# TensorE's six middle attention batches written out one after another instead of looping on the engine

## The chip, the cores and the metric

The kernel runs on one core of a Trainium2 chip. A core has a matrix engine (TensorE, PE in the profile, with a row of its own, PEld, for its weight loads), a vector engine (VectorE, DVE), a scalar engine (ScalarE, ACT), a general engine (GpSimd, POOL) and an engine that issues transfers (SyncE, SP). Each runs its own program and they meet through semaphores. Every engine fetches its instructions from memory, over DMA queues that the profile lists as kind "instruction". The metric is the device time of one execution in microseconds (us); lower is better.

## The reference, cut to what matters

Eight batches of 256 tokens with 512 features pass through one decoder layer: causal attention with 32 query heads in 8 groups, a mixing stage over a second input with long convolutions, and a gated feed-forward stage with ternary weights.

```python
def reference(x, ctx_2048, ...):
    x = x + _L0_attn_ref(_layernorm(x), Wq, Wk, Wv, Wo, bo)
    x = x + _L0_xattn_ref(ctx_2048, ctx_2048, _layernorm(x), ssm_kernel, D, 8)
    x = x + _L0_ffn_ref(_layernorm(x), w_gate_up, w_proj)
    return x

# the attention
q = _rope((h @ Wq).reshape(N, S, 32, 64).transpose(0, 2, 1, 3))
k = _rope((h @ Wk).reshape(N, S, 8, 64).transpose(0, 2, 1, 3))
v = (h @ Wv).reshape(N, S, 8, 64).transpose(0, 2, 1, 3)
scores = (q @ k.T + alibi) / math.sqrt(64)
scores = 30.0 * jnp.tanh(scores / 30.0)
probs = jax.nn.softmax(jnp.where(causal, scores, -jnp.inf), axis=-1)
return (probs @ v) @ Wo + bo
```

## The kernel before

Every engine's program has three stages in a row: attention, mixing, feed-forward. Attention takes up the first 690 us and goes batch by batch. In each engine's program batch 0 is written out (`first_batch`), batches 1 to 6 are one body `attend(b)` in a loop on the engine (`Fori(1, B - 1)`, B is 8), and batch 7 is written out again (`last_batch`). A loop on the engine means that the body's instructions stand in memory once, a register counts, and a compare-and-branch at the end goes back to the head.

TensorE's body for batch b has ten steps, one for each of the eight head groups and two more:

- steps 0 and 1: the values of this batch (`project_values`, at L701 to L703 with the tile `hT_halves` as stationary side, shown as `bank<-w_hi,hT_halves`), each followed by the scores of a head group (`scores`, L779 and L782);
- steps 2 to 4: the last three of the batch's ten projections of keys and queries ("units", `project`, L701 to L703, shown as `bank<-hT_halves,w_hi`), a head group's scores, and the weighting of values for the head group two steps before (`values`, L789, L791, with the softmax sums at L814 and L816);
- steps 5 to 9: the output projection of a head group (`output`, L701 to L703 on `ctx_hi`), with scores and values as long as there are any;
- then the first seven units of batch b + 1, with the last three output projections between them. So the next batch's operands are under way when the next pass of the body begins.

What TensorE waits for in the body: `ctx_lo` (GpSimd, L2002, its last piece of a head group's context) before an output projection, `hT_in` (transposing transfers that SyncE issues at L605, from `parts` to `hT_halves`) before the first unit of the next batch, and for the scores `unit_turned` (VectorE, L1443 to L1446, the rotation of a unit), `unit_in` (the unit's transfers into `q_both`, `q_high`, `k_high`, `k_low`) and `tanh_done`.

GpSimd has the longest list per head group: it masks the exponentials (L1989), adds key sums (L1998), adds a unit's rotated parts (L1984) and makes `ctx_lo` (L2002). VectorE quantises a share of the feed-forward weights beside the attention: L1574 before the end of the body, L1579 to L1583 in step 0, L1590 in step 2.

Inside the loop a wait's target depends on the batch, so it comes from a register; the program holds small register instructions for it. Two later stages also loop on TensorE: the mixing at L987 and the feed-forward at L1104.

Of the kernel before, what the change touches and what calls it, by code (L numbers as in the profile page):

```python
# [35 lines left out]
B, S, D = 8, 256, 512  # L36
# [53 lines left out]
def decoder_layer(nc, x, ctx_pairs, wq, wk, wv, wo, bo, kern, dcoef, w_gu, w_p, rope_cos, rope_sin, key_bias, query_bias,  # L90
# [17 lines left out]
    with ExitStack() as stack:  # L108
# [587 lines left out]
        def _(pe):  # L696
# [143 lines left out]
            def attend(b):  # L840
                for step in range(STEPS):
                    filler(b, step)
                    if step < NG:
                        scores(b, step)
                    if step >= 2:
                        values(b, step - 2, False)
                pe.wait_ge(tanh_done, NG * (b + 1))
                left = range(STEPS - WO_AFTER, NG)
                for n in range(EARLY):
                    project(b + 1, n)  # L850
                    if n < len(left):
                        output(b, left[n])
# [95 lines left out]
                        output(0, g)  # L948

            first_batch()  # L950
            with pe.Fori(1, B - 1) as b:
                attend(b)
            last_batch()

# [1263 lines left out]
```

## Time and profile before

| | before |
|---|---|
| median of 3 runs | 1197.77 us (1191.97 to 1198.88) |
| the profiled execution | 1198.49 us |
| span in its profile | 1196.8 us |
| PE busy | 1139.7 us, 95% |
| PEld busy | 810.7 us, 68% |
| DVE busy | 876.6 us, 73% |
| POOL busy | 676.9 us, 57% |
| ACT busy | 553.8 us, 46% |
| mean granted TensorE clock | 0.987 |

The span is the stretch from the first to the last instruction of the profiled execution, and 1.7 us of its time lie around it. Times inside the trace count from the span's start. "Issue" as a releaser means that the engine waited for nothing that the profile shows. The granted clock is 1.0 for 2.4 GHz and 0.5 for 1.2 GHz; a stretch that has some of both shows a value between.

### The profile page before, as it was taken

To read this page: it belongs to the slowest core of one execution; us is meant where nothing else is said; L and a number is where in the kernel's file an instruction comes from. 1 tells how busy PE (TensorE), PEld (TensorE's weight loads), DVE (VectorE), ACT (ScalarE), POOL (GpSimd) and SP (SyncE) were. 2 spreads that over 40 slices of the span, in tenths; PEclk is the share of its full clock that TensorE was granted. 3 is DMA by queue.
4 is the path that set the end of the run, shared out by engine and by line. 5 is a ranking of instruction groups with operands and counts; after the bars stand their busy time and mean duration, and the time that the engine had idled before them with its cause. 6 is when DMAs were issued, how large, how long until landed. Compare 5 with 4: busy or idle time off the path is not lost. (4 is left out here: it accounts for less than half of the span.)

```text
span 1196.8 us, 27182 instructions
## 1 busy us (share of the span) xinstructions
PE 1139.7 (95%) x10867; PEld 810.7 (68%) x10882; DVE 876.6 (73%) x1287; ACT 553.8 (46%) x617; POOL 676.9 (57%) x557
## 2 busy tenths in 40 slices
PE   5998999999999999999999999999999999999998
PEld 4665557656666666566566577777786876786683
DVE  6979788687786886886878678888746645754654
ACT  6866564653754655646546500000244533542441
POOL 1553594674764945946749769999443322422331
PEclk9999999999999999999999999999999999999999
DMA  9572454464345344634544557774001222012000
GB/s 329 151 226 81 120 173 110 131 181 129 109 148 173 99 145 147 182 111 121 163 128 131 213 96 147 145 144 92 1 19 21 34 54 53 7 45 53 19 19 36
DMA packets 166191, 134.28 MB, mean 112 GB/s; under 512 B 69628, under 2 KB 127362, under 8 KB 166082
## 3 DMA queue, kind: packets, MB, share of 16 engines
q1 hardware_dynamic: 141128, 126.44, 37.0%
q10 hardware_dynamic: 24960, 6.29, 3.6%
q8 instruction: 86, 1.41, 0.5%
q14 instruction: 17, 0.14, 0.0%
HBM read 81.76 MB, written 35.21 MB: 98 GB/s over the span
## 5 line engine op out<-in xcount | busy, mean ns | idle before, releaser
L701 PE MATMUL bank<-hT_halves,w_hi 128*128 128x256 f16 x640 | 176.6, 276 | 10.4 <-DMA hT_halves<-parts 5.8
L1984 POOL TENSOR_TENSOR parts<-parts 128x512 f32<-128x512 f32 x80 | 119.2, 1493 | 105.7 <-DVE parts L1446 105.7
L703 PE MATMUL bank<-hT_halves,w_lo 128*128 128x256 f16 x640 | 176.3, 276 | 0.0
L702 PE MATMUL bank<-hT_halves,w_hi 128*128 128x256 f16 x640 | 176.3, 275 | 0.0
L963 PE MATMUL bank<-kv,toep 128*128 128x288 f32 (+2 forms) x660 | 157.8, 401 | 0.7 <-ACT qT L1211 0.5
L963 PEld LDWEIGHTS bank<-kv,toep 128*128 128x128 f32 x660 | 123.7, 190 | 34.0 <-ACT qT L1211 0.7
L2002 POOL TENSOR_TENSOR ctx_lo<-ctx,ctx_hi 128x512 f16<-128x512 f32 x64 | 105.9, 1654 | 66.2 <-ACT ctx_hi L1153 66.1
L1174 ACT ACTIVATE region_c<-bank,cap_scale 128x1536 f32<-128x1536 f32 x64 | 98.6, 1541 | 86.4 <-PE bank L782 86.0
L1989 POOL TENSOR_SCALAR_AFFINE_SELECT region_c<-region_c 128x512 f32<-128x512 f32 x128 | 86.0, 695 | 85.4 <-ACT region_c L1177 85.2
L2132 POOL TENSOR_TENSOR sqsum<-sqsum,toep 128x512 f32<-128x512 f32 x56 | 78.0, 1393 | 95.5 <-ACT toep L1353 95.3
L1041 PE MATMUL bank<-odd_halves,guT 128*128 128x256 f16 x512 | 112.2, 273 | 0.0
L1042 PE MATMUL bank<-odd_halves,guT 128*128 128x256 f16 x512 | 112.2, 273 | 0.0
L1041 PE MATMUL bank<-cpair,guT 128*128 128x256 f16 x496 | 108.8, 273 | 0.3 <-DVE hid L1863 0.3
L1042 PE MATMUL bank<-cpair,guT 128*128 128x256 f16 x496 | 108.8, 273 | 0.0
L1159 ACT CAST halves<-parts 128x512 f16<-128x512 f32 x80 | 49.2, 615 | 123.8 <-POOL parts L1984 119.4
L701 PE MATMUL bank<-region_o,ctx_hi 128*128 128x512 f16 x256 | 97.6, 381 | 6.9 <-POOL ctx_lo L2002 6.9
L1365 ACT ACTIVATE silu<-bank 128x512 f32<-128x512 f32 x64 | 38.1, 595 | 142.0 <-PE bank L1042 138.7
L1998 POOL TENSOR_TENSOR key_sum<-region_c 128x512 f32<-128x512 f32 x56 | 98.8, 1764 | 1.8
L1598 DVE TENSOR_TENSOR halves<-parts,halves 128x512 f16<-128x512 f32 x80 | 68.1, 851 | 40.5 <-ACT halves L1159 40.4
L702 PE MATMUL bank<-region_o,ctx_hi 128*128 128x512 f16 x256 | 97.3, 380 | 0.0
L703 PE MATMUL bank<-region_o,ctx_lo 128*128 128x512 f16 x256 | 97.1, 379 | 0.0
L1177 ACT ACTIVATE region_c<-region_c 128x1536 f32<-128x1536 f32 x64 | 95.1, 1485 | 2.0
(192 smaller groups left out, 2637.0 us busy)
## 6 DMA issues: line engine op xcount, KB each, us to landing
unit_halves<-halves SPq DMA_DIRECT2D x80, 256.0 KB, 2.4
q_both<-unit_halves SPq DMA_DIRECT2D x64, 256.0 KB, 2.9
q_high<-unit_halves SPq DMA_DIRECT2D x64, 128.0 KB, 3.1
toep<-kernel_padded SPq DMA_DIRECT2D x32, 256.0 KB, 4.0
wffn<-w_gu SPq DMA_DIRECT2D x6, 1280.0 KB, 6.7
cpair<-ctx_pairs SPq DMA_DIRECT2D x32, 176.0 KB, 4.8
xin<-x SPq DMA_DIRECT2D x8, 512.0 KB, 4.1
region_o<-wq SPq DMA_DIRECT2D x4, 1024.0 KB, 11.2
```

Of the source, the lines that this page charges most:

```text
L701: pe.matmul(dst, lh, rh, start=first and k == 0, stop=False)
L702: pe.matmul(dst, lh, rl, start=False, stop=False)
L703: mm = pe.matmul(dst, ll, rh, start=False, stop=last and k == n - 1)
L963: mm = pe.matmul(dst, toep[:, n, d * P:(d + 1) * P], kv[:, p, m * B + batches.start:m * B + batches.stop, :], start=(m == 0), stop=(m == l))
L1041: pe.matmul(dst, guT[:, k, col:col + P], h3_hi[p][:, k, :], start=(k == 0), stop=False)
L1042: mm = pe.matmul(dst, guT[:, k, col:col + P], h3_lo[p][:, k, :], start=False, stop=(k == DB - 1))
L1174: act.activation(s.rearrange("p (n c) -> p n c", n=3), bank[:, 0:3, :], ACT.Tanh, scale=cap_scale[:, g // 2:g // 2 + 1]).then_inc(tanh_don ...
L1177: act.activation(s, s, ACT.Exp, scale=CAP).then_inc(exp_done, 1)
L1984: pool.tensor_tensor(slot[:, 0], slot[:, 0], slot[:, 1], ALU.add).then_inc(unit_summed, 1)
L1989: last = pool.affine_select(s, s, pattern=[[0, REP], [sign, P]], compare_op=ALU.is_ge, fill=0.0, base=0, channel_multiplier=-sign)
L1998: pool.tensor_tensor(key_sum[:, g % 2], sc_first[:, g % 3, :, P:S], sc_second[:, g % 3], ALU.add).then_inc(keys_added, 1)
L2002: pool.tensor_tensor(ctx_lo[:, 2 * g:2 * g + 2, :], ctx32[:, g % 2], ctx_hi[:, 2 * g:2 * g + 2, :], ALU.subtract).then_inc(ctx_lo_done, 1)
```

## The change

```diff
@@ -948,7 +948,7 @@
             first_batch()
-            with pe.Fori(1, B - 1) as b:
+            for b in range(1, B - 1):
                 attend(b)
             last_batch()
```

`b` is now a Python number, so the body is written into TensorE's program six times, and every wait gets a constant. The instructions of the other four engines are the same, in the same order; each of them still loops. TensorE's matmuls and their order are the same too.

At the end of the body, TensorE before: the last matmuls of the seventh unit of the next batch, the loop's counter and branch, and behind them the first values matmuls of `last_batch`.

```order
L701 MATMUL bank<-hT_halves,w_hi 128x256
L702 MATMUL bank<-hT_halves,w_hi 128x256
L703 MATMUL bank<-hT_halves,w_lo 128x256
L951 REGISTER_ALU
L951 COMPARE_AND_BRANCH
L701 MATMUL bank<-w_hi,hT_halves 128x512 [waits wo_undone]
L702 MATMUL bank<-w_lo,hT_halves 128x512
```

The same place in TensorE's program of the change, between batches 1 and 2:

```order
L701 MATMUL bank<-hT_halves,w_hi 128x256
L702 MATMUL bank<-hT_halves,w_hi 128x256
L703 MATMUL bank<-hT_halves,w_lo 128x256
L701 MATMUL bank<-w_hi,hT_halves 128x512 [waits wo_undone]
L702 MATMUL bank<-w_lo,hT_halves 128x512
```

The counter and the branch are gone; the next batch's first matmul stands directly behind.

At the first scores of a batch, TensorE, the difference between the two programs:

```order
 L703 MATMUL bank<-w_hi,hT_halves 128x512
-L755 ISA
-L756 REGISTER_ALU [waits unit_in0]
-L760 ISA [waits unit_in1]
-L779 MATMUL bank<-q_both,k_high 32x2x160 [waits unit_turned]
+L779 MATMUL bank<-q_both,k_high 32x2x160 [waits unit_turned,unit_in1,unit_in0]
 L779 MATMUL bank<-q_both,k_high 32x2x192
```

The register instructions that worked out and carried waits are gone, and the matmul itself carries them all.

## Rows read from the trace of the kernel before

**Rows 1.** Page, part 1: busy time, share, instructions of TensorE.

```profile
PE 1139.7 (95%) x10867; PEld 810.7 (68%) x10882; DVE 876.6 (73%) x1287; ACT 553.8 (46%) x617; POOL 676.9 (57%) x557
```

**Rows 2.** Waits of TensorE: line, releaser: us in total, times, longest.

```profile
PE bank L701 <- issue: 12.9, 5, 2.9
...
PE bank L701 <- POOL ctx_lo L2002: 6.9, 10, 1.4
PE bank L701 <- DMA hT_halves<-parts: 5.8, 6, 2.1
```

**Rows 3.** Branches of TensorE's three loops: ns min/median/max, first and last start us.

```profile
L951 PEldq COMPARE_BRANCH  x6: 83/4242/4757, 207.5 to 619.4; - x6
...
L987 PEldq COMPARE_BRANCH  x6: 76/208/233, 726.2 to 823.2; - x6
...
L1104 PEldq COMPARE_BRANCH  x2: 76/144/211, 1005.9 to 1090.3; - x2
```

**Rows 4.** Timeline of TensorE, end of batch 3: start us, us, instruction, idle before.

```profile
373.35 0.27 PE L703 MATMUL bank<-hT_halves,w_lo 128*128 128x256 f16 x1
376.55 0.61 PE L701 MATMUL bank<-w_hi,hT_halves 128*128 128x512 f16 x1 [2.92 <-issue]
```

**Rows 5.** Windows at the five loop-backs: us, busy PE PEld DVE ACT POOL, clock, DMA.

```profile
209.31:211.78 2.47, 0.16 (x2) 0.00 (x1) 2.47 (x5) 0.62 (x1) 0.58 (x2) 1.00 0.41 126
...
536.36:539.05 2.69, 0.17 (x2) 0.00 (x1) 1.95 (x4) 0.62 (x1) 1.76 (x2) 1.00 0.54 136
sum 13.69, PE 0.82 PEld 0.02 DVE 10.28 ACT 3.09 POOL 8.17; mean PE 0.16 PEld 0.00 DVE 2.06 ACT 0.62 POOL 1.63
```

**Rows 6.** Windows, batches 1 to 7, from first values matmul to end of second scores.

```profile
130.66:138.26 7.60, 7.60 (x74) 3.74 (x73) 7.49 (x7) 3.52 (x3) 0.47 (x1) 1.00 0.49 135
211.78:221.08 9.30, 9.29 (x73) 4.15 (x74) 5.96 (x5) 4.13 (x4) 1.81 (x2) 0.82 0.84 252
295.11:304.01 8.90, 8.90 (x73) 4.08 (x74) 5.75 (x4) 4.13 (x4) 0.75 (x2) 0.85 0.86 265
376.55:385.65 9.10, 9.10 (x72) 4.10 (x72) 5.75 (x4) 4.13 (x4) 0.62 (x2) 0.83 0.81 255
457.59:466.89 9.30, 9.30 (x73) 4.14 (x74) 5.75 (x4) 4.13 (x4) 1.29 (x2) 0.82 0.80 254
539.05:548.25 9.20, 9.20 (x72) 4.07 (x72) 5.75 (x4) 4.13 (x4) 1.02 (x2) 0.81 0.76 235
621.19:628.79 7.60, 7.60 (x75) 3.73 (x73) 5.48 (x7) 4.64 (x5) 2.82 (x3) 1.00 0.72 213
```

**Rows 7.** Windows, batches 1 and 3, from first values matmul to next batch's first unit.

```profile
130.66:183.19 52.53, 50.27 (x734) 31.69 (x732) 43.61 (x64) 34.64 (x31) 40.98 (x36) 1.00 0.51 141
295.11:347.33 52.22, 51.51 (x732) 32.01 (x732) 39.73 (x60) 35.24 (x32) 39.07 (x37) 0.97 0.53 158
```

**Rows 8.** Waits of TensorE within 130 to 211 us (batch 1).

```profile
PE bank L701 <- POOL ctx_lo L2002: 1.3, 2, 1.1
PE bank L701 <- DMA hT_halves<-parts: 0.9, 1, 0.9
```

**Rows 9.** Waits of TensorE within 295 to 376 us (batch 3).

```profile
PE bank L701 <- POOL ctx_lo L2002: 0.4, 1, 0.4
PE bank L701 <- DMA hT_halves<-parts: 0.3, 1, 0.3
```

**Rows 10.** Timeline of GpSimd, first masks and key sums, batches 1 and 3.

```profile
137.79 3.32 POOL L1989 TENSOR_SCALAR_AFFINE_SELECT region_c<-region_c 128x512 f32<-128x512 f32 x2 [11.44 <-ACT region_c L1177]
...
303.55 1.22 POOL L1989 TENSOR_SCALAR_AFFINE_SELECT region_c<-region_c 128x512 f32<-128x512 f32 x2 [8.15 <-ACT region_c L1177]
```

**Rows 11.** DMA queue of instructions: count, MB, share; branch 371.62:376.38, batch 295.11:376.55, loop 706:823.

```profile
q8 instruction: 1, 0.02, 1.3%
...
q8 instruction: 9, 0.15, 0.8%
...
q8 instruction: 1, 0.02, 0.1%
```

**Rows 12.** Timelines at the loop's exit: VectorE's seventh rotation, TensorE's first scores after.

```profile
622.33 0.41 DVE L1446 TENSOR_TENSOR parts<-bank,sin_s 128x256 f32<-128x256 f32 x1
...
623.87 0.67 PE L779 MATMUL bank<-q_both,k_high 128*32 128x320 f16 x12
```

## The prediction

> **What bounds the kernel now.** I began with the busy times on the page. TensorE is busy 95% of the span, the next engine, VectorE, 73% [rows 1]. So time goes away only where TensorE idles or works at the lower clock, and the second view is the list of its waits. The largest entry in it is not a wait for another engine: 12.9 us in 5 pieces, released by "issue", each before a matmul at L701 [rows 2]. Five is the number of times that a loop of six passes goes back to its head.
>
> The third view confirms the place. The loop's branch at L951 was executed six times, 83 ns at the least and 4242 ns at the median. The two other loops of TensorE have branches of 76 to 233 ns [rows 3]. Six passes mean five taken branches and one that falls through, so I read the five long ones as taken and the 83 ns one, at 619.4 us, as the exit. The timeline at the end of batch 3 shows what reaches the array: the last matmul of the seventh unit starts at 373.35 and the next batch's first one at 376.55, with 2.92 us idle [rows 4]. TensorE had work queued, which hides part of each branch; the rest is the gap.
>
> Why this branch is long can be read from the instruction queue, at least in part. While the branch of batch 3 was pending, one block of instructions was fetched; a whole batch fetches nine, for all engines together; the loop at L987, whose body is short, needed one over its whole 117 us [rows 11]. So the attention body is fetched anew in each pass, and at the branch its head has to come from memory before anything can be issued. The short loop's body stays where it is.
>
> **What the change does, part by part.** First, it removes the branch. The gap itself, counted from where the next matmul would have started at the normal distance, is 2.47 us at the first loop-back and 2.69 us at the last, and 13.69 us over all five [rows 5]. I take that sum and not the 12.9 us of the waits, since those count from the matmuls' modelled ends.
>
> The nearest row for the price of the boundary without a loop-back is the loop's exit. There the same matmuls follow each other from the loop's last pass into `last_batch`, and the first values and scores of batch 7 take 7.60 us with nothing between [rows 6]. The change makes the five other boundaries like it. Removal: −13.7 us, if nothing that was hidden behind the gap becomes late.
>
> What could be late is the seventh unit. Scores of the next batch wait for its rotation. At the exit, the rotation's last piece ends at 622.33 + 0.41 = 622.74, and the first scores start at 623.87 [rows 12]: 1.1 us to spare without any gap. The value projection covers it. I add nothing. That projection lasts 623.87 − 621.19 = 2.7 us [rows 6, 12]; without it the scores would come 1.6 us too early, but it stays where it is.
>
> Second, the clock. In batches 2 to 6, the first values and scores take 9.30, 8.90, 9.10, 9.30 and 9.20 us, at a mean granted clock of 0.81 to 0.85; in batches 1 and 7, which no gap precedes, 7.60 us at 1.00 [rows 6]. So after each gap TensorE runs for a while at the lower of its two levels, 1.2 GHz, and loses 1.7 + 1.3 + 1.5 + 1.7 + 1.6 = 7.8 us in all. The gap is the only thing the five have in front of them and the two have not, so the drop should go with it.
>
> Is that 7.8 us a gain? Here I compare batch 1, which starts without a gap, with batch 3, which starts slow. From the first values matmul to the first unit of the next batch, batch 1 takes 52.53 us at clock 1.00 and batch 3 takes 52.22 us at 0.97 [rows 7]. The head start of 1.3 us is gone by then. It went into waits: batch 1 waits 1.3 us for `ctx_lo` and 0.9 us for the transposed inputs, batch 3 0.4 and 0.3 us [rows 8, 9]. The difference is 1.5 us, which is the head start. GpSimd explains the first part: its first two masks take 3.32 us in batch 1 and 1.22 us in batch 3 [rows 10], because in batch 1 they come while VectorE is still in its quantising steps. The wait for the inputs is that for a chain over VectorE, GpSimd, ScalarE and a transfer, which does not start earlier because TensorE's first matmuls were quick. With the gap gone, VectorE's quantising stands relative to TensorE where it stands in batch 1. So I book the clock at nothing: 7.8 us less work for TensorE, 7.8 us more waiting. Bounds: 0 and −7.8 us.
>
> Third, the register instructions before waits. They are issued by the sequencer while the array has work queued. Batch 7, written out with constants, and batch 1, in the loop with registers, both take 7.60 us for the same matmuls [rows 6]. That includes the place shown in the program's difference. Price: 0.
>
> Fourth, the code. It grows by five bodies, but TensorE executes no more instructions than before, and a body was fetched in each pass already [rows 11]. No wait on "issue" stands anywhere in TensorE's list in the middle of a body; all are at the loop-backs [rows 2]. So sequential fetching keeps up with this stream. Price: 0.
>
> The sum: 1198.49 − 13.7 = 1184.8 us for the profiled execution. That one lies 0.7 us above the median of the runs, so the median should come to 1197.77 − 13.7 = **1184.1 us**.
>
> One rule speaks against all this. The Trainium skill, page "Advanced Engine Details and Errata", section "Control Flow Timing", puts a compare-and-branch at about 108 ns; by it five of them would be worth an estimated 0.5 us, and the time would be 1197.2 us. The branches at L987 and L1104 bear it out and L951 does not, at 4242 ns. The page "Runtime: NRT & Kernel Launch", section "Instruction fetch mechanics", says that a taken branch to code which is not held forces a fetch before execution goes on, and that fetching in sequence is mostly hidden. By that rule, the trace agrees for L951, and it gives the same sum as mine.
>
> **The rivals.**
>
> (B) The clock's 7.8 us are gained as well. For it: TensorE is the busiest engine, and every step moves on with it; the 0.9 us wait for inputs in batch 1 may be chance, since such waits vary up to 2.1 us [rows 2]. Against: batch 1 [rows 7]. Time: 1184.1 − 7.8 = 1176.3 us.
>
> (C) The gap's time comes back as waits for the inputs. TensorE waits for the transposed inputs in all six batches, 5.8 us in total and 2.1 us at the most [rows 2]. They share the DMA engines with the loads of weights and with stores. If each of the six waits came to 2.1 us, that would be 12.6 − 5.8 = 6.8 us more: 1190.9 us. For it: all six already wait, so there is no slack there. Against: those transfers are issued behind work that is itself counted from the batch's start.
>
> (D) The change doesn't do what it says: the pause sits at the batch boundary for another reason than the branch, and stays. That gives 1197.8 us, or 1197.3 us with the branch's own 0.1 us each taken off. Against it: the exit at 619.4 us is the same boundary without a pause [rows 3, 6].
>
> (E) Slower: the written-out code is fetched too late. If each of 9 fetches in five batches [rows 11] stopped TensorE as long as a loop-back does on average, 13.69 / 5 = 2.7 us, it would cost 45 × 2.7 = 123 us, and the time would be 1198 − 14 + 123 = 1307 us. It decides from 13.7 / 45 = 0.30 us per fetch on. Against it: the body passes as many fetches now with no wait on "issue" in between.
>
> **How the numbers follow.** Forecast (A) 0.60, (B) 0.15, (C) 0.18, (D) 0.05, (E) 0.02. The likeliest case gives the time, 1184.1 us, and its own spread is about ±3 us, as input waits and single clock drops fall differently in each execution. The range goes from just above (B) to near (C): 1177 to 1190 us. It leaves out (D), (E), the far half of (B) and the end of (C), which is less than 2 in 10. A measurement of this kernel can tell about 1% from no change, which is 12.0 us, so the border lies at 1185.8 us. Of (A) three quarters are below it, 0.45; with (B)'s 0.15 and 0.02 of (C), faster is 0.62. The rest of (A), 0.15, of (C), 0.16, and (D) make 0.36 for within 1%. Slower is 0.02.
>
> **What would show it.** In the changed profile, TensorE's list has no "issue" wait at L701 from 130 to 620 us: that is step one. The first values and scores of every batch take 7.6 us at clock 1.00: step two. The waits for `ctx_lo` and for the inputs in batches 2 to 6 rise together by some 7 us, and each batch takes about 209.31 − 130.66 = 78.65 us from values to values, as batch 1 does up to its gap [rows 5, 6]: step three. The count of instruction fetches is about as before and none stops TensorE: step four. The prediction is wrong if "issue" waits show up inside the written-out batches, if input waits of 2 us stand in nearly every batch, or if batches take 77 us because the clock's share is kept.

## The result, and the profile after

The changed kernel takes 1186.58 us, median of six runs (1181.91 to 1190.98), against 1195.47 us for six runs of the kernel before. The ratio is 0.992, with a 95% interval from 0.990 to 0.995: 0.8% or 9.3 us less by the ratio, 8.9 us by the two medians. A second measurement gave 1185.36 us and 0.993 (0.990 to 0.995). So it is faster beyond the measurement's uncertainty, but by less than 1%, which the forecast held to be the less likely case (0.36 against 0.62). The forecast was 13.7 us less, 1184.1 us, in a range from 1177 to 1190.

The page of the changed kernel, busy times. TensorE's share is 95% as before [rows 1], in a span of 1184.8 us:

```profile
PE 1131.4 (95%) x10882; PEld 810.0 (68%) x10882; DVE 881.1 (74%) x1287; ACT 553.0 (47%) x617; POOL 687.7 (58%) x557
```

TensorE's waits in the changed kernel, whole program (line, releaser, us in total, times, longest):

```profile
PE bank L701 <- POOL ctx_lo L2002: 12.5, 14, 1.6
...
PE bank L701 <- DMA hT_halves<-parts: 8.3, 6, 2.8
```

The entry of L701 on "issue" is gone. The other two were 6.9 and 5.8 us [rows 2]: 8.1 us of waiting have come up in their place.

Windows of the changed kernel over the first values and scores of batches 1, 2, 3 and 7 (us, busy PE, PEld, DVE, ACT, POOL, granted clock, DMA share, GB/s). They answer to [rows 6]:

```profile
132.97:140.57 7.60, 7.60 (x74) 3.73 (x73) 7.50 (x7) 3.52 (x3) 0.46 (x1) 1.00 0.48 142
211.17:218.77 7.60, 7.60 (x74) 3.70 (x71) 5.68 (x8) 4.26 (x5) 1.93 (x2) 1.00 0.76 226
292.39:299.99 7.60, 7.60 (x75) 3.74 (x73) 5.47 (x7) 4.65 (x5) 2.83 (x3) 1.00 0.89 273
609.01:616.61 7.60, 7.60 (x75) 3.74 (x73) 5.47 (x7) 4.65 (x5) 2.82 (x3) 1.00 0.71 209
```

All are alike, at the full clock, and so are batches 4 to 6, which also take 7.60 us each. The same view from a batch's first values matmul to the next batch's first unit, batches 1 to 6; it answers to [rows 7]:

```profile
132.97:185.06 52.09, 50.24 (x733) 31.80 (x732) 43.58 (x64) 34.59 (x31) 40.99 (x36) 1.00 0.48 141
211.17:266.29 55.12, 50.22 (x735) 31.78 (x733) 44.15 (x65) 35.99 (x33) 44.02 (x39) 1.00 0.57 162
292.39:345.26 52.87, 50.25 (x734) 31.78 (x732) 41.92 (x64) 35.75 (x33) 43.52 (x38) 1.00 0.59 173
371.37:424.63 53.26, 50.22 (x735) 31.73 (x733) 43.88 (x65) 35.97 (x33) 43.75 (x39) 1.00 0.57 167
450.73:503.22 52.49, 50.24 (x735) 31.81 (x732) 41.89 (x64) 35.71 (x33) 43.50 (x38) 1.00 0.59 168
529.33:582.91 53.58, 50.23 (x735) 31.81 (x732) 45.92 (x65) 36.27 (x33) 44.43 (x39) 1.00 0.54 170
```

From the first values matmul of batch 1 to that of batch 7 it is 609.01 − 132.97 = 476.0 us, against 621.19 − 130.66 = 490.5 us before [rows 6]. Between the two profiled executions that stretch gave 14.5 us, more than forecast. Yet the medians differ by 8.9 us. The experiments are about this difference.

### The profile page after: what moved, and what is told of

Its sections match the earlier page's. It is cut to its first block and busy times, and to the rows that moved or that the text cites. A ratio compares the mean times of both kernels' runs of the same rounds, so it can differ in the third digit from the quotient of the medians.

```text
span 1184.8 us, 27046 instructions
## 1 busy us (share of the span) xinstructions
PE 1131.4 (95%) x10882; PEld 810.0 (68%) x10882; DVE 881.1 (74%) x1287; ACT 553.0 (47%) x617; POOL 687.7 (58%) x557
## 5 line engine op out<-in xcount | busy, mean ns | idle before, releaser
L701 PE MATMUL bank<-hT_halves,w_hi 128*128 128x256 f16 x640 | 176.6, 276 | 13.5 <-DMA hT_halves<-parts 8.3
L1984 POOL TENSOR_TENSOR parts<-parts 128x512 f32<-128x512 f32 x80 | 118.2, 1480 | 107.6 <-DVE parts L1446 107.6
L1989 POOL TENSOR_SCALAR_AFFINE_SELECT region_c<-region_c 128x512 f32<-128x512 f32 x128 | 106.2, 854 | 60.2 <-ACT region_c L1177 60.2
L701 PE MATMUL bank<-region_o,ctx_hi 128*128 128x512 f16 x256 | 97.6, 381 | 12.5 <-POOL ctx_lo L2002 12.5
L1598 DVE TENSOR_TENSOR halves<-parts,halves 128x512 f16<-128x512 f32 x80 | 71.4, 892 | 49.2 <-ACT halves L1159 48.8
L1998 POOL TENSOR_TENSOR key_sum<-region_c 128x512 f32<-128x512 f32 x56 | 90.7, 1620 | 1.8
```

Source lines behind the costliest of these rows:

```text
L701: pe.matmul(dst, lh, rh, start=first and k == 0, stop=False)
L1984: pool.tensor_tensor(slot[:, 0], slot[:, 0], slot[:, 1], ALU.add).then_inc(unit_summed, 1)
L1989: last = pool.affine_select(s, s, pattern=[[0, REP], [sign, P]], compare_op=ALU.is_ge, fill=0.0, base=0, channel_multiplier=-sign)
L1998: pool.tensor_tensor(key_sum[:, g % 2], sc_first[:, g % 3, :, P:S], sc_second[:, g % 3], ALU.add).then_inc(keys_added, 1)
```

## Experiments

### The same two kernels again

No edit.

> The changed kernel once more, to settle its size and to get a second profile. Theory A (the gaps alone are gained, 13.7 us, and the difference to the measured 9 us is chance in the first batch and in the input waits, which is the same in both kernels): ratio 0.986 to 0.992, the stretch from the first values matmul of batch 1 to that of batch 7 takes 474 to 480 us again (490.5 us before, 476.0 us in the first profile of the change), and no 'issue' wait at a batch boundary. Rival (the longer program costs something outside the loop, in batch 0, where the first profile shows batch 1 starting 2.3 us later): batch 1 starts at 133 us again, where the kernel before has it at 130.7 us.

Measured: 1185.36 us (1185.11 to 1188.01), ratio 0.993 (0.990 to 0.995). The stretch from batch 1 to batch 7 takes 474.5 us. Batch 1 starts at 133.00 us.

> The kernel before once more, for a second profile. Theory A: five gaps of 2.4 to 3.2 us with a branch of 4 to 5 us at L951, in all 13 to 15 us; the stretch from batch 1 to batch 7 takes 488 to 494 us. If the start of batch 1 varies by chance, it lies anywhere from 130 to 134 us; by the rival (the longer program costs batch 0 some 2 us) it stays within 0.5 us of 130.7 us.

Measured: one execution, 1193.51 us. Batch 1 starts at 135.10 us, so later than in the changed kernel: batch 0 varies by chance, and the rival on it falls. The stretch to batch 7 takes only 481.3 us, 9.2 us less than in the first profile of the same kernel and below the expected 488. The gaps, expected at 13 to 15 us in all, are 12.8 us.

Windows of this second execution over the five loop-backs, which answer to [rows 5], their sum:

```profile
sum 12.84, PE 0.83 PEld 0.03 DVE 9.25 ACT 2.51 POOL 8.81; mean PE 0.17 PEld 0.01 DVE 1.85 ACT 0.50 POOL 1.76
```

The gaps are nearly as long as in the first one, 13.69 us. Where the time differs is shown by the windows from first values matmul to the next batch's first unit, batches 2 to 6:

```profile
215.68:266.58 50.90, 50.21 (x732) 31.67 (x732) 40.42 (x61) 35.85 (x33) 40.05 (x37) 1.00 0.57 173
295.15:346.03 50.88, 50.21 (x732) 31.67 (x733) 39.87 (x60) 35.40 (x32) 39.75 (x37) 1.00 0.54 165
375.12:427.70 52.58, 51.89 (x733) 32.12 (x733) 39.77 (x60) 35.30 (x32) 39.09 (x37) 0.97 0.53 158
456.42:509.01 52.59, 51.89 (x732) 32.10 (x733) 39.83 (x60) 35.35 (x32) 39.46 (x37) 0.97 0.51 161
537.59:590.28 52.69, 50.21 (x732) 31.68 (x733) 41.10 (x60) 35.62 (x32) 40.64 (x38) 1.00 0.54 161
```

The clock dropped behind two of the five gaps only, in batches 4 and 5. Batches 2 and 3 have a gap and no drop, which the first profile never showed, and they take 50.9 us, 1.7 us less than batches with both. (The last one has no drop either, but waited 2.1 us for its inputs.) So behind a gap a drop costs 1.7 us. What the gap itself gives back is read against batches with neither gap nor drop. Batch 1 is one in each profile of the kernel before, and it takes 52.5, 52.1 and, in the third execution below, 52.2 us: 1.2 to 1.6 us more than 50.9. The changed kernel, without gaps, gets 52.1 us at best. In the twelve such batches of its two profiles, with what an input wait exceeds 0.3 us taken off, it is 51.7 to 52.6 us, 52.15 on the average. So a gap gives back some 1.2 us within the batch.

The timelines of GpSimd and VectorE show why. GpSimd at the start of batch 2 of this execution (start us, us, instruction, idle before):

```profile
222.82 1.94 POOL L1989 TENSOR_SCALAR_AFFINE_SELECT region_c<-region_c 128x512 f32<-128x512 f32 x2 [6.59 <-ACT region_c L1177]
...
226.60 1.22 POOL L1989 TENSOR_SCALAR_AFFINE_SELECT region_c<-region_c 128x512 f32<-128x512 f32 x2 [0.49 <-ACT region_c L1177]
```

VectorE there, the end of its quantising:

```profile
221.66 2.02 DVE L1583 TENSOR_TENSOR wffn<-wffn,region_c 128x3584 bf16<-128x3584 bf16 x1
```

The changed kernel, batch 3, GpSimd and then VectorE:

```profile
299.53 3.53 POOL L1989 TENSOR_SCALAR_AFFINE_SELECT region_c<-region_c 128x512 f32<-128x512 f32 x2 [3.85 <-ACT region_c L1177]
...
304.37 3.02 POOL L1989 TENSOR_SCALAR_AFFINE_SELECT region_c<-region_c 128x512 f32<-128x512 f32 x2
```

```profile
300.23 2.33 DVE L1583 TENSOR_TENSOR wffn<-wffn,region_c 128x3584 bf16<-128x3584 bf16 x1
...
304.15 2.16 DVE L1590 TENSOR_TENSOR wffn<-wffn 128x3584 bf16<-128x3584 bf16 x1
```

Counted from the batch's first values matmul, the masks start at 7.1 us in both. VectorE's L1583 ends at 8.0 us with the gap ahead and at 10.2 us without: during the gap VectorE goes on. Two pairs of masks take 1.94 + 1.22 = 3.2 us in the one and 3.53 + 3.02 = 6.6 us in the other. GpSimd is behind from there on, and TensorE meets that at `ctx_lo`.

The traces bear this out in every batch. The first four masks of a batch take 2.5 to 3.3 us together wherever a gap or a pause stands in front of it, with a clock drop or without: 27 batches in six profiles. In batches 1 to 6 without one they take 6.3 to 6.6 us, in nine profiles of kernels that quantise at this place. A single mask takes 0.62 to 0.65 us with VectorE idle and 2.4 to 2.5 us beside L1583 or L1590, and it ends some 0.5 us behind the end of VectorE's operation: above, L1583 ends at 302.56 and the pair of masks at 303.06. It is held up until then, rather than slowed evenly.

TensorE's waits inside the attention loop close the account. Second execution of the kernel before, 130 to 616 us:

```profile
PE bank L701 <- issue: 12.0, 5, 2.8
PE bank L701 <- DMA hT_halves<-parts: 3.6, 6, 2.1
PE bank L701 <- POOL ctx_lo L2002: 3.4, 7, 1.1
```

Changed kernel, 130 to 608 us:

```profile
PE bank L701 <- POOL ctx_lo L2002: 8.8, 11, 1.2
PE bank L701 <- DMA hT_halves<-parts: 8.3, 6, 2.8
PE bank L701 <- ACT v_s L1121: 0.8, 2, 0.4
```

The changed kernel's second profile has 8.9 us for `ctx_lo` and 6.6 us for inputs. From the second execution of the kernel before to the first profile of the change, gone are the gaps, 12.8 us, and two drops at 1.7 us. Come are 5.4 us for `ctx_lo`, 4.7 us for inputs and 0.8 us for the values. That is −16.2 + 10.9 = −5.3 us, and the stretches are 481.3 and 476.0 us.

### The kernel before a third time

> The kernel before a third time, for one more draw of where the clock drops fall. Theory P: for each batch from 2 to 6, the stretch from the previous batch's first unit to its own first unit is 28.5 to 29.2 us (26.1 plus the pause) and then 50.9 us where no drop falls behind the pause, 52.2 to 52.7 us where one does, plus what an input wait over 0.6 us adds; so the stretch from batch 1 to batch 7 follows the number of drops n as about 478 + 1.6 n us plus long input waits. Rival A (no link between drop and stretch): batches without a drop take 52.5 us too.

Measured: one execution, 1195.78 us; drops behind three of the five gaps, stretch 485.5 us. Windows of batches 2 to 5:

```profile
214.51:265.42 50.91, 50.21 (x733) 31.69 (x733) 39.80 (x60) 35.34 (x32) 39.61 (x37) 1.00 0.54 166
293.85:346.40 52.55, 51.89 (x733) 32.01 (x733) 40.06 (x60) 35.57 (x32) 39.75 (x37) 0.97 0.52 161
375.18:426.29 51.11, 50.21 (x733) 31.68 (x733) 40.04 (x60) 35.59 (x32) 39.40 (x37) 1.00 0.54 166
454.95:507.53 52.58, 51.89 (x732) 32.07 (x733) 39.81 (x60) 35.35 (x32) 39.51 (x37) 0.97 0.52 161
```

Batches without a drop take 50.9 and 51.1 us, those with one 52.6 us, as theory P says; rival A, 52.5 us in both, falls. The formula gives 478 + 3 × 1.6 = 482.8 us. The rest is batch 6, which waited 2.0 us for inputs and had another drop, 1.7 us, behind that wait at 591.7 us; the two are a little more than the missing 2.7 us. With 5, 2 and 3 drops behind gaps, the three stretches are 490.5, 481.3 and 485.5 us, 485.8 us on average; the two profiles of the change average 475.3 us. The difference, 10.5 us, is close to the 8.9 and 10.3 us between the medians of the two measurements (9.3 and 8.7 us by the ratios).

### Loops of one pass

```diff
-            with pe.Fori(1, B - 1) as b:
-                attend(b)
+            for k in range(1, B - 1):
+                with pe.Fori(k, k + 1) as b:
+                    attend(b)
```

> Six copies of the body, but each in an engine loop of one pass: registers, address arithmetic and register waits as before, no taken branch back. Theory A (the taken branch is all; registers cost nothing): no gap over 0.5 us at the boundaries, time as the changed kernel within 2 us, 1183 to 1190 us. Rival (register waits or the loop set-up carry a part of it): time between both kernels, 1189 to 1195 us, with idle time at the head of each copy.

Measured: 1186.91 us (1184.14 to 1188.22), ratio 0.993 (0.991 to 0.995). Its branches (ns min/median/max):

```profile
L952 PEldq COMPARE_BRANCH  x6: 74/74/93, 207.8 to 606.5; - x6
```

No gap at the boundaries, and the ratio of the change (0.992 and 0.993). The registers and their waits cost nothing that can be measured; the taken branch is the whole effect, within the 0.2 to 0.3% of the intervals.

### Two batches per pass

```diff
-            with pe.Fori(1, B - 1) as b:
-                attend(b)
+            with pe.Fori(0, B // 2 - 1) as i:
+                attend(2 * i + 1)
+                attend(2 * i + 2)
```

> Three passes of a body with two batches: the branch is taken twice in place of five times. Theory A (each taken branch of this size costs its 2.7 us, the rest is absorbed): two gaps of 2.4 to 3.2 us, before batches 3 and 5, and two clock drops; time above the changed kernel by 2 x 2.7 = 5.5 us, and below the one before by 8.2 us or, if the change as measured is scaled (9 us for five), by 5.4 us: 1186 to 1191 us. Rival (the pause belongs to batch boundaries): five gaps, time as before, 1195 us.

Measured: 1190.89 us (1183.96 to 1193.96), ratio 0.996 (0.994 to 0.998). Branch and waits of TensorE:

```profile
L951 PEldq COMPARE_BRANCH  x3: 83/4821/5623, 290.3 to 611.7; - x3
```

```profile
PE bank L701 <- issue: 6.8, 2, 3.8
```

Two pauses stand at the two loop-backs and none at the boundaries inside the body: 3.15 us before batch 3 and 4.0 us before batch 5, longer than expected. The batch behind the first of them had no drop and took 50.9 us; only the second pause had a drop, where two were expected. About half of the change's gain is there with two of the five branches left.

This run has batches with and without a pause in one execution. GpSimd's first masks in batch 3, behind a pause, and in batch 4, behind a boundary without one:

```profile
302.38 1.23 POOL L1990 TENSOR_SCALAR_AFFINE_SELECT region_c<-region_c 128x512 f32<-128x512 f32 x2 [7.01 <-ACT region_c L1178]
...
379.36 3.53 POOL L1990 TENSOR_SCALAR_AFFINE_SELECT region_c<-region_c 128x512 f32<-128x512 f32 x2 [3.85 <-ACT region_c L1178]
```

### A shorter body

```diff
                 for k, ((lh, ll), (rh, rl)) in enumerate(pairs):
                     pe.matmul(dst, lh, rh, start=first and k == 0, stop=False)
-                    pe.matmul(dst, lh, rl, start=False, stop=False)
-                    mm = pe.matmul(dst, ll, rh, start=False, stop=last and k == n - 1)
+                    mm = pe.matmul(dst, lh, rl, start=False, stop=short[0] and last and k == n - 1)
+                    if not short[0]:
+                        mm = pe.matmul(dst, ll, rh, start=False, stop=last and k == n - 1)
```

`short[0]` is true for the loop's body alone.

> The kernel before, with the third product of each split product left out of the loop's body (units, values and output projections), so that a pass executes 1679 instructions on TensorE in place of 1919; only the branch is looked at. Theory A (the body does not fit what the engine holds, and its head is fetched anew): if 1679 still doesn't fit, branches of about 4 us and gaps as before, and a block of instructions fetched at each; if it fits, branches of 0.2 us as at L987 and L1104 (1312 instructions), no gap, and fewer instruction fetches in the whole run. Rival (the branch is long because of what the loop's registers or waits do): about 4 us at any length of the body.

Measured: 1174.33 us in one execution, which has less work and is no comparison. Its branches, and the count of instruction fetches in the whole run, first here and then in the kernel before:

```profile
L955 PEldq COMPARE_BRANCH  x6: 76/207/243, 207.6 to 592.0; - x6
```

```profile
q8 instruction: 40, 0.66, 0.2%
...
q8 instruction: 86, 1.41, 0.5%
```

The taken branch costs 207 to 243 ns, no gap, and fetches fall from 86 to 40. The loop, its registers and its kinds of waits are the same; the length differs, and with it the matmuls left out. (From one branch to the next the traces have 1683 and 1923 instructions of TensorE; the difference is the same 240.) So between 1679 and 1919 instructions lies, in this kernel, the length up to which TensorE goes back to the head at once. That it keeps the body is inferred from the short branch and the fewer fetches; those are counted for all engines together. The changed kernel needs 78 fetches.

### A pause without a branch

```diff
             for b in range(1, B - 1):
+                if b > 1:
+                    pe.wait_ge(unit_summed, UNITS * b + EARLY)
                 attend(b)
```

> The written-out program with a pause of another kind put back at the five boundaries: TensorE waits there until GpSimd has added the seventh unit's parts, some 3.3 us after the first values matmul would have started. No branch and no fetch. Theory P (a pause gives VectorE's quantising a head start over GpSimd's masks, which is worth about 1.7 us in the same batch, 52.6 to 50.9 us from first values matmul to the next batch's first unit; a clock drop right after the pause takes that away): pauses of 3.2 to 3.4 us, batches without a drop at 50.9 us, those with a drop at 52.2 to 52.7 us; time above the changed kernel by 5 x (3.2 - 1.7) = 7.5 us without drops to 5 x 3.2 = 16 us with five: 1193 to 1202 us. Rival A of the prediction (a pause costs its length whatever the clock does): 16 us, and the batches stay at 52.5 us with or without a drop. Rival F (the fetch is what hurts, not the pause): time as the changed kernel.

Measured: 1207.35 us (1201.39 to 1208.46), ratio 1.008 (1.005 to 1.011), so 1.6% or 19 us above the changed kernel, beyond the expected 1202 us. TensorE's waits, 130 to 628 us:

```profile
PE bank L701 <- POOL parts L1986: 16.5, 5, 3.7
PE bank L701 <- DMA hT_halves<-parts: 7.4, 6, 2.9
PE bank L701 <- POOL ctx_lo L2004: 3.5, 7, 1.2
```

The wait for `ctx_lo` is back at 3.5 us, as in the kernel before, with a pause of another cause. Batch 6, which had no drop and no long input wait, took 50.89 us from values to unit; batch 3, with a drop, 52.95 us. That is theory P's mechanism, with one reservation: this pause ends when GpSimd has finished its sum, so GpSimd's lead is built into it. The theory's sum was short: the pauses were 3.0 to 3.9 us, 17.3 us in all, not 3.2 to 3.4, and there were longer drops than counted (batch 4, at a clock of 0.95, took 54.3 us) and one behind an input wait. Rival F falls: the pause costs without any fetch.

### VectorE's quantising earlier, with and without the loop

```diff
                 for step in range(STEPS):
-                    if step == 0:
-                        find_below(b - 1)
...
                             output(b, i)
+                find_below(b)
                 low_unit(b + 1, EARLY - 1)
```

The same is done in batches 0 and 7.

> The written-out program with one move on VectorE: the three operations L1579 to L1583 of a share's quantising go from the start of a batch to just before the last operation of the seventh unit, where VectorE waits some 1.9 us for ScalarE. Theory P (the waits for ctx_lo in the changed kernel come from GpSimd's first masks running beside this quantising): first masks of a batch 1.2 to 1.9 us in place of 3.6 us, 50.9 to 51.3 us from first values matmul to the next batch's first unit in place of 52.6, waits for ctx_lo down from 12.5 to about 7 us, time 5 to 6 times 1.3 to 1.7 us less: 1176 to 1180 us. Rival W (the waits belong to the chain of transfers): first masks quicker, but the time stays, with longer waits for the transposed inputs: 1184 to 1187 us.

Measured: 1182.95 us (1180.70 to 1185.87), ratio 0.988 (0.986 to 0.990). GpSimd's first two pairs of masks in batch 3 (L1987 here):

```profile
302.21 2.75 POOL L1987 TENSOR_SCALAR_AFFINE_SELECT region_c<-region_c 128x512 f32<-128x512 f32 x2 [3.85 <-ACT region_c L1177]
...
306.29 3.06 POOL L1987 TENSOR_SCALAR_AFFINE_SELECT region_c<-region_c 128x512 f32<-128x512 f32 x2
```

TensorE's waits, 130 to 609 us:

```profile
PE bank L701 <- DMA hT_halves<-parts: 7.8, 6, 2.8
PE bank L701 <- POOL ctx_lo L2000: 5.8, 7, 1.2
```

The time lies between theory P's 1176 to 1180 and rival W's 1184 to 1187 us. The wait for `ctx_lo` fell from 8.8 to 5.8 us, and the ratio is some 0.5% below the change's. But the first masks only went from 3.53 to 2.75 us, not to 1.9: moved forward, L1579 takes 3.09 us in place of 2.02, beside GpSimd's sum of parts (L1984, here L1982), and the quantising still ends 1.2 us after the masks begin. Batches 1, 3, 4 and 5 took 52.0 to 52.3 us where 50.9 to 51.3 was expected, with 0.4 to 1.0 us of input wait among it; batches 2 and 6 waited 2.8 and 1.8 us for inputs and took 54.3 and 53.3 us: part of rival W. With what the input wait exceeds 0.3 us taken off, batches 2 to 6 come to 51.3 to 51.8 us, and their first four masks take 5.8 to 5.9 us. Both numbers lie between those of a batch with a gap and those of the changed kernel, the first with some overlap.

> The same move on VectorE in the kernel before, with the loop on TensorE. Theory P: here the quantising is out of the masks' way with or without the pause, so a pause has nothing left to give back and costs its full 2.4 to 3.1 us, plus what drops cost: 50.9 us per batch to the next first unit where no drop falls, and up to 52.5 us where one does; the kernel is 13 to 16 us slower than the written-out one with the same move (against 9 us between the two kernels of the change), so 1190 to 1194 us. Rival A: the difference to the written-out one with the move is the same 9 us as without it.

Measured: 1192.13 us (1189.94 to 1199.46), ratio 0.998 (0.995 to 1.001). The difference to the written-out kernel with the same move is 1.0% or 12 us by the ratios, 9.2 us by the medians. That lies between theory P's 13 to 16 us and rival A's 9 us and doesn't decide. Its profile has drops behind two of the five gaps; those two batches took 52.7 us, and of the three others two took 50.9 us and one, with an input wait of 1.8 us, 52.4 us. Theory P's premise failed as well: with the same move a batch behind a gap takes 50.9 us and the written-out one at least 51.3, because only the gap takes the quantising fully out of the masks' way. Their first four take 2.5 us here.

### The residual's load behind the transposes

```diff
-                next_residual(b, 4 * TT * b + 2 * TT)
                 turn_rows(b + 1)
+                next_residual(b, 4 * TT * b + 2 * TT)
```

> The written-out program with one move on SyncE: the residual's load of 0.5 MB is issued behind the two transposing transfers of the next inputs in place of ahead of them. Theory T (TensorE's wait for the transposed inputs, 6.6 to 8.3 us in six batches, is their queueing behind the loads of weights and residual): that wait falls to 3 to 5 us and the time by 2 to 4 us, to 1181 to 1184 us. Rival S (the wait is set by when VectorE, GpSimd and ScalarE have the rows ready, and by the transfer's own 2 us): no change, 1184 to 1187 us.

Measured: 1183.22 us (1178.03 to 1183.73), ratio 0.991 (0.987 to 0.994). TensorE's waits, 130 to 605 us:

```profile
PE bank L701 <- POOL ctx_lo L2002: 8.4, 11, 1.2
PE bank L701 <- DMA hT_halves<-parts: 3.5, 6, 1.3
```

The input wait fell from 8.3 us (6.6 us in the change's second profile) to 3.5 us and the other stayed, as theory T says; the stretch to batch 7 takes 470.7 us. That speaks against rival S for the wait, on one profile each; the same move in the next run left 5.6 us. For the time, the interval overlaps that of the change, so no gain is shown there.

> Written-out program, VectorE's quantising ahead of the seventh unit's last operation, and the residual's load behind the transposes. If the two moves add: quant_first's 3 us less than the changed kernel and residual_late's 2 to 4 us, 1178 to 1181 us, with 51 to 51.6 us from first values matmul to the next batch's first unit. If quant_first was already held by the input wait, as its profile suggests (1.1 to 1.3 us in most batches), the sum is larger than the parts: down to 1176 us. If the load is not in the way: 1182 to 1184 us.

Measured: 1180.33 us (1177.61 to 1181.95), ratio 0.989 (0.987 to 0.991). It is the lowest median, but the kernel before was quicker on that occasion (1192.94 us), and by ratio it is level with quant_first. The two moves don't add up in a way that can be measured: the wait for `ctx_lo` is 6.5 us and that for inputs 5.6 us, 2.1 us of it in one batch.

## Why the prediction was off in size

**What held.** The kernel is faster and within the range. The cause is the taken branch at L951, and the five gaps are gone with TensorE's matmuls and their order unchanged. The price of the register instructions, 0, holds (loops of one pass). Fetching in sequence holds: 78 fetches, no "issue" wait in 130 to 608 us. The seventh unit was no problem: every batch starts with 7.60 us. The waits for `ctx_lo`, inputs and values rose by 5.4 + 2.5 + 0.8 = 8.7 us against the first profile; the forecast was some 7 us. Against that profile the whole account closes: 13.7 us of gaps, 7.8 us of drops behind them and 1.7 us of the drop at 594.7 us are gone and 8.7 us of waits have come, 14.5 us in all. Of the rivals, (B), (D) and (E) did not come. (C) came in part: the input wait grew by 2.5 us in all against the first profile and 4.7 us against the second, and in the worst batch from 2.1 to 2.8 us. The rule that opens the rivals was held to be borne out by the branches at L987 and L1104. That is only roughly so: those that were taken lasted 208 to 233 ns, about twice its 108 ns, and those that fell through 76 ns [rows 3].

**The step that failed** is the one that booked the removal at the full 13.7 us and the clock drops at nothing. Its comparison was batch 1, without gap and without drop, against batch 3, with both: 52.53 and 52.22 us [rows 7]. From that I read that nothing is gained when the drops go. In fact three things nearly cancelled. Batch 3 had some 1.0 us from the gap, through VectorE and GpSimd, and an input wait shorter by 0.6 us; its drop took 1.3 us away. The case that tells them apart, a gap without a drop, was absent in the one profile I had: all five gaps had a drop behind them [rows 6]. In three other profiles of kernels with these five loop-backs (before_again, before_third, loop_quant_first) it is 2, 3 and 2 of five.

A gap also shortens the input waits. What they exceed 0.3 us by comes to 4.8 to 6.6 us in three profiles without gaps and to 2.0 to 4.1 us in the three of the kernel before, some 0.6 us per gap. So, as an estimate from these numbers, 1.2 + 0.6 = 1.8 us of a gap comes back. A loop-back costs 2.7 + 1.7 − 1.8 = 2.6 us with a drop and 2.6 − 1.8 = 0.8 us without. With 12 drops in 20 gaps, five loop-backs cost 5 × (0.6 × 2.6 + 0.4 × 0.8) = 9.4 us, close to the measured 8.9 and 10.3 us (9.3 and 8.7 by the ratios). That drops cost time is seen without profiles too. In the 45 further executions of the kernel before that were timed beside the runs, the time rises by 0.7 us, with a standard error of 0.2 us, for each us lost at the lower clock, (1 − granted clock) × time. If drops cost nothing, it would be 0. This is a correlation, and a coarse one: the clock is on record to 0.001, which is 1.2 us.

**The correction to the median** failed with it. I put the profiled execution 0.7 us above the median and took the sum over as it stood. That execution has the most drops behind gaps of the three profiles, and, as the third has, a drop behind an input wait besides. Its stretch from batch 1 to batch 7 is 4.7 us above the average of the three, 490.5 against 485.8 us; its start of batch 1, at 130.7 us, came 2.3 us early, 133.0 us being the average, and hid a part of that. The median of 19 further runs of the kernel before is 1195.6 us, 2.9 us below the profiled one.

**The term for the batch** was 78.65 us from values to values. It is 78.2 to 79.7 us in five batches and 81.2 us in the second, which waited 2.8 us for its inputs; the mean is 79.3 us.

What stays open: why the drop comes behind some gaps of 2.3 to 3.1 us and not behind others. The length doesn't decide it: in the third execution a gap of 2.3 us had one and a gap of 3.1 us none.

## What to carry to other kernels

A loop on TensorE was free here only with a body short enough to be kept. So read the branch's own row: 0.2 us went with no gap, 4 to 5.6 us with a head that had to be fetched. If it was fetched, write the loop out or shorten the body. Before a pause is booked as a gain, ask what the other engines do in it, and compare cases that differ in one condition only; if the profile has no such case, profile the same kernel again.

## What the runs showed of the hardware

- A taken branch on TensorE took 207 to 243 ns with a body of 1679 instructions and 3.95 to 4.76 us with a body of 1919 and 4.8 and 5.6 us with one of two batches; one that falls through takes 74 to 93 ns.
- Behind the same gap of 2.3 to 3.1 us, TensorE went on at 2.4 GHz in 8 of 20 cases and at 1.2 GHz for a while in 12. A drop cost 1.3 to 1.7 us. Behind input waits of 2.0 to 2.9 us it came in 5 of 10 cases, in the profiles other than that of the short body.
- GpSimd's mask takes 0.62 to 0.65 us alone and 2.4 to 2.5 us beside VectorE's 128x3584 bf16 operations L1583 and L1590, until some 0.5 us behind their end; VectorE's L1579 took 3.09 us in place of 2.02 beside GpSimd's L1984 (L1982 in that run).
- The same kernel's time to the start of batch 1 varied from 130.7 to 135.1 us between three executions.
